# Projection and attention of an AdaLN block in one program block, with constant rows set four at a time

## What is computed

```
# B = 8 batches, C = 512 channels, T = 1024 tokens, H = 16 heads of 32
Q, K, V = proj(Wq), proj(Wk), proj(Wv)          # y = einsum('oc,bct->bto', W, x)
att = einsum('bhqd,bhkd->bhqk', Q, K) / sqrt(32) + b[0]
att = att * m + (1.0 - m) * -1e30               # m masks keys
y = softmax(att) @ V                            # (B, C, T) after transposes
q, in_scale = per_token_quant_int8(y)           # a "token" is a channel row of 1024
out = (q @ weight.T) * in_scale * w_scale + bias
x = x + out.astype(float16)
```

## Time and profile before

| | |
|---|---|
| median of 3 executions | 2441.13 us (2439.86 to 2441.28) |
| the profiled execution's own time | 2436.68 us |
| its span, first to last instruction | 2434.8 us |
| TensorE busy | 2381.2 us, 98% |
| GpSimd, VectorE, ScalarE busy | 1673.1, 1560.6, 1347.4 us |
| mean granted TensorE clock | 0.993 of 2.4 GHz |

### The profile page before, as it was taken

One profiled execution on the slowest core, in us unless ns is written; L12 is line 12 of the kernel. 1 busy time (PEld: TensorE's weight loads), 2 busy tenths in 40 slices (PEclk: granted clock), 3 DMA queues, 4 the chain that ended last, 5 costly groups with the idle time before them and its releaser, 6 DMA issues.

```text
span 2434.8 us, 37355 instructions
## 1 busy us (share of the span) xinstructions
PE 2381.2 (98%) x12344; PEld 1343.4 (55%) x12376; DVE 1560.6 (64%) x1683; ACT 1347.4 (55%) x2536; POOL 1673.1 (69%) x677
## 2 busy tenths in 40 slices
PE   8999999997999999999999999999999999999996
PEld 7888888884444444444444444444444444444442
DVE  3311111145777787777777777777777777777771
ACT  3322222214666666666666666666666666666664
POOL 3322223414788888888778888887888888888777
PEclk9999999998999999999999999999999999999999
DMA  6655555365677766776777776766776667766751
GB/s 242 255 193 205 211 195 196 149 211 131 149 160 159 159 148 153 161 158 154 156 158 160 156 161 152 159 148 154 158 161 156 153 151 160 159 155 152 157 111 46
DMA packets 143498, 396.55 MB, mean 163 GB/s; under 512 B 14584, under 2 KB 50424, under 8 KB 127296
## 3 DMA queue, kind: packets, MB, share of 16 engines
q0 software_dynamic: 18144, 132.13, 27.4%
q10 hardware_dynamic: 48864, 129.19, 22.0%
q1 hardware_dynamic: 76416, 134.34, 15.1%
HBM read 161.51 MB, written 100.93 MB: 108 GB/s over the span
## 4 chain that ended last, share of the span: by engine, by line
PE 64%; DMA 6%; issue 2%; DVE 2%; POOL 2%; SPq 0%; ACT 0%; ACTq 0%; POOLq 0%; DVEq 0%
PE score L724 21%; PE pv L751 18%; PE ring L128 17%; DMA q_stack<-max_lo 5%; PE ring L784 4%; PE ring L763 2%; PE ring L766 2%; DVE neg_max L137 1%; DMA k_stack<-bias_part 1%; PE ring L775 1%; POOL acc L1014 1%; DMA probs<-probs 0%; PE ring L144 0%; POOL acc L1026 0%; SPq L165 0%
## 5 line engine op out<-in xcount | busy, mean ns | idle before, releaser
L832 ACT ACTIVATE probs<-score 128x512 f32<-128x512 f32 x2048 | 1075.3, 604 | 583.2 <-PE score L724 570.3
L137 DVE TENSOR_REDUCE neg_max<-ring 128x1 f32<-128x1024 f32 x1024 | 1208.6, 1220 | 236.7 <-PE ring L128 225.1
L724 PE MATMUL score<-q_stack,k_stack 100*128 100x512 f32 x2048 | 875.4, 429 | 12.3 <-ACT probs L832 5.5
L1014 POOL TENSOR_TENSOR acc<-acc,probs 128x2048 f32<-128x2048 f32 x189 | 866.9, 4587 | 25.2 <-DMA probs<-probs 10.5
L128 PE MATMUL ring<-k_stack,q_stack 98*128 98x512 f32 x2048 | 810.6, 396 | 12.8 <-DMA k_stack<-bias_part 12.5
L724 PEld LDWEIGHTS score<-q_stack,k_stack 100*128 100x128 f32 x2048 | 387.4, 189 | 492.2 <-ACT probs L832 357.6
L751 PE MATMUL pv<-probs,v_in 128*32 128x512 f32 x4096 | 546.3, 605 | 0.0
L128 PEld LDWEIGHTS ring<-k_stack,q_stack 98*128 98x128 f32 x2048 | 390.7, 191 | 79.1 <-DMA k_stack<-bias_part 12.8
L1014 POOL TENSOR_TENSOR acc<-probs 128x2048 f32<-128x2048 f32 x63 | 289.0, 4588 | 105.0 <-DMA probs<-probs 105.0
L526 POOL TENSOR_TENSOR q_stack<-x_raw,k_stack 128x1024 fp32r<-128x1024 f32 x28 | 67.7, 2455 | 293.1 <-ACT k_stack L402 293.1
L998 POOL DMA_DIRECT2D probs<-probs x126 | 108.7, 863 | 170.2 <-PE pv L751 163.3
(11 more groups left out here) (101 smaller groups left out, 2028.9 us busy)
## 6 DMA issues: line engine op xcount, KB each, us to landing
probs<-probs POOLq DMA_DIRECT2D x126, 1024.0 KB, 8.0
q_stack<-qk_part ACTq DMA_DIRECT2D x183, 256.0 KB, 4.5
k_stack<-qk_part ACTq DMA_DIRECT2D x90, 512.0 KB
qk_part<-part_hi SPq DMA_DIRECT2D x64, 512.0 KB, 2.6
qk_part<-part_lo SPq DMA_DIRECT2D x64, 512.0 KB, 3.5
v_steps<-v_out SPq DMA_DIRECT2D x64, 256.0 KB, 2.2
v_out<-x ACTq DMA_DIRECT2D x32, 512.0 KB, 5.7
out<-v_out SPq DMA_DIRECT2D x64, 256.0 KB, 2.0
```

Source lines behind the costliest of these rows:

```text
L137: nc.vector.tensor_reduce(neg_max[:, pair // CHUNK, pair % CHUNK:pair % CHUNK + 1], ring[:, :], AX_X, ALU.max, negate=True).then_inc(neg_m ...
L724: pe.matmul(score[score_bank(t)][:, :], k_stack[par][0:ROWS, h, kt * P:(kt + 1) * P], q_stack[par][0:ROWS, half, h, :], start=True, stop=T ...
L832: nc.scalar.activation(probs[:, kt, h, :], score[score_bank(t)][:, :], ACT.Exp).then_inc(exp_done, 1)
L1014: nc.gpsimd.tensor_tensor(acc[:, half, :, :], first, probs[:, tile, :, :], ALU.add).then_inc(acc_done, 1)
```

## The change

Both parts are now written into one block, so the barrier between them is gone. What it ordered is ordered by semaphores: SyncE, VectorE and GpSimd begin attention with a wait for the last projection group (`proj_done`), ScalarE, VectorE and GpSimd with one for the last stores of `qk_part`; the first three score matmuls wait for `v_done`, and `V_BANKS` is turned so that bank 0 is the first to be free. `set_rows` writes rows 96 to 99 only, K's first, and the loads of rows 0 to 95 do not wait for it; the bias loads wait for K's rows. The load of V for step 0 is issued with the loads of step 0, before batch 7's stores; for this `v_in` exists throughout, and the projection's `w_raw` is a view of it.

```diff
@@ set_rows
-    nc.gpsimd.memset(q_stack[:, :, :, :].bitcast(F32), LIFT).then_inc(stack_set, 1)
-    nc.gpsimd.memset(k_stack[:, :, :].bitcast(F32), 1.0).then_inc(stack_set, 1)
+    nc.gpsimd.memset(k_stack[ROW_BIAS:ROWS, :, :].bitcast(F32), 1.0).then_inc(stack_set, 1)
+    nc.gpsimd.memset(q_stack[ROW_BIAS:ROWS, :, :, :].bitcast(F32), LIFT).then_inc(stack_set, 1)
@@ project
-        w_raw = sb("w_raw", [P, CT, C], F32)
+        w_raw = v_in[:, :, :, :].rearrange("p i a c -> p (i a c)").rearrange("p (a c) -> p a c", a=CT)
-        V_BANKS = (0, 1, 2)
+        V_BANKS = tuple((bank + SCORES - TT) % SCORES for bank in range(SCORES))
-        block = ctx.enter_context(nc.Block())
@@ project, SyncE, before batch 7
-            sp.wait_ge(stack_set, 2)
+            sp.wait_ge(proj_done, GROUPS * (B - 1))
             for k in range(3):
                 load_q(sp, qk_d, q_stack, 0, 0, 0, k, q1_loaded)
             for k in range(3):
                 load_k(sp, qk_d, k_stack, 0, 0, k, k_loaded)
+            sp.wait_ge(stack_set, 1)
             for part in range(2):
                 load_bias(sp, bias_d, k_stack, 0, 0, part, k_loaded)
             for k in range(3):
                 load_q(sp, qk_d, q_stack, 0, 0, 1, k, q2_loaded)
+            sp.wait_ge(fw_done, 1)
+            for i in range(2):
+                sp.wait_ge(v_stored[i], 16 * (B - 1) * TT // 2)
+            sp.dma_start(v_in[:, 0, :, :], v_d[0]).then_inc(v_loaded[0], 16)
             batch(B - 1, 1, last=True)
-            for i in range(2):
-                sp.wait_ge(part_stored[i], 32 * B * STAGES // 2)
@@ project, GpSimd, before batch 7
                     pool.wait_ge(proj_done, GROUPS * b)
+                    pool.wait_ge(k_lo_done, TT * b)
                     set_rows(nc, q_stack[0], k_stack[0], stack_set)
+                    pool.wait_ge(stack_set, 2)
@@ attend, SyncE
-            sp.dma_start(v_in[:, 0, :, :], v_d[0]).then_inc(v_loaded[0], 16)
-            sp.wait_ge(stack_set, 4)
+            sp.wait_ge(proj_done, PROJECTED)
             for k in range(3):
                 load_q(sp, qk_d, q_stack, 1, 1, 0, k, q1_loaded)
             for k in range(3):
                 load_k(sp, qk_d, k_stack, 1, 1, k, k_loaded)
+            sp.wait_ge(stack_set, 3)
@@ attend, TensorE
+                if isinstance(s, int) and s == 0 and t < SCORES:
+                    pe.wait_ge(v_done, B * TT - SCORES + 1 + t)
+                    if isinstance(own, int) and (own, pair) == (1, 0):
+                        pe.wait_ge(stack_set, 4)
@@ attend, ScalarE
-                if s == 0 and t == 24:
-                    act.wait_ge(stack_set, 4)
+            for i in range(2):
+                act.wait_ge(part_stored[i], 16 * B * STAGES)
@@ attend, GpSimd
+            pool.wait_ge(proj_done, PROJECTED)
+            for i in range(2):
+                pool.wait_ge(part_stored[i], 16 * B * STAGES)
             set_rows(nc, q_stack[1], k_stack[1], stack_set)
+            pool.wait_ge(stack_set, 4)
```

More of the change, by code:

```diff
@@ L68 @@
 MAX_ROWS = 16 * 2
+GROUPS = 3 * TT
+STAGES = 2 * CT
+PROJECTED = GROUPS * B
 def wait(eng, sem, value):
@@ L170, in project @@
             stack_set, k_loaded, q1_loaded, q2_loaded, rowmax_done, neg_max_done,
-            ident_set, maxT_done, max_hi_done, max_lo_done, max_rows):
+            ident_set, maxT_done, max_hi_done, max_lo_done, max_rows,
+            block, sems, v_in, v_loaded, proj_done, part_stored, v_done, fw_done):
     QHI, QLO, KHI, KLO = range(4)
@@ L209, in project @@
         k_lo_done = sem("k_lo_done")
-        v_done = sem("v_done")
-        part_stored = [sem(f"part_stored{i}") for i in range(2)]
         small_loaded = sem("small_loaded")
@@ L359, in batch @@
                 if last:
+                    pe.wait_ge(stack_set, 2)
                     pe.wait_ge(k_loaded[0], LOADS_K)
@@ L905, in _ @@
         def _(dve):
+            dve.wait_ge(proj_done, PROJECTED)
+            for i in range(2):
+                dve.wait_ge(part_stored[i], 16 * B * STAGES)
             nc.vector.memset(ones[:, :], 1.0).then_inc(const_set, 1)
@@ L1095, in program @@
         banks = score + [buf[:, half * N:(half + 1) * N] for buf in ring for half in range(2)] + [pv]
-        stack_set, rowmax_done, neg_max_done, ident_set, maxT_done, max_hi_done, max_lo_done = (
+        stack_set, rowmax_done, neg_max_done, ident_set, maxT_done, max_hi_done, max_lo_done, proj_done, v_done, fw_done = (
             ctx.enter_context(nc.semaphore(name)) for name in
-            ("stack_set", "rowmax_done", "neg_max_done", "ident_set", "maxT_done", "max_hi_done", "max_lo_done"))
-        k_loaded, q1_loaded, q2_loaded, max_rows, v_stored = (
+            ("stack_set", "rowmax_done", "neg_max_done", "ident_set", "maxT_done", "max_hi_done", "max_lo_done",
+             "proj_done", "v_done", "fw_done"))
+        k_loaded, q1_loaded, q2_loaded, max_rows, v_stored, v_loaded, part_stored = (
             [ctx.enter_context(nc.semaphore(f"{name}{i}")) for i in range(2)]
-            for name in ("k_loaded", "q1_loaded", "q2_loaded", "max_rows", "v_stored"))
+            for name in ("k_loaded", "q1_loaded", "q2_loaded", "max_rows", "v_stored", "v_loaded", "part_stored"))
+        sems = ctx.enter_context(ExitStack())
+        block = ctx.enter_context(nc.Block())
         shared = (banks, ring, q_stack, k_stack, neg_max, max_hi, max_lo, ident, v_out, v_stored,
                   stack_set, k_loaded, q1_loaded, q2_loaded, rowmax_done, neg_max_done,
-                  ident_set, maxT_done, max_hi_done, max_lo_done, max_rows)
+                  ident_set, maxT_done, max_hi_done, max_lo_done, max_rows,
+                  block, sems, v_in, v_loaded, proj_done, part_stored, v_done, fw_done)
         project(nc, x, mask, wqT, wkT, wvT, qk_d, v_d, bias_d, cond_b, fw, wT, ws_rep, fb_rep, w_scale, f_bias, *shared)
```

16 lines of the change are left out of this document (6 added, 10 removed).

## The result

The changed kernel takes 2426.36 us in the median (2425.51 to 2428.83, 5 executions) against 2439.86 us before (2438.3 to 2441.28, 5 executions): ratio 0.9947, 95% interval 0.9932 to 0.9961, 13.5 us less. The forecast was 2428.1 us, a gain of 13.0 us on the median of 2441.13 us known then.

A forecast was written before the change was run, and what follows sets the result against it. TensorE, busy 2381.2 of 2434.8 us, was taken as the bound; the border held 18.95 us, less a 3.6 us wait and 2.3 us dip gives 13.0 us gained, so 2428.1 us, own range 2425 to 2431, with A and B 2422 to 2434.7.

The forecast's parts named there:

- The border: Between projection and attention: idle time and half-clock stretches of TensorE hold 18.95 us, all this change can win.
- The barrier, 1.75 + 1.5 us: Between the two parts: removal gains 1.75 us of TensorE idling and 1.5 us of half clock behind it.
- Issue of the loads at 557.3: SyncE's first load of step 1 moves from 564.66 to about 557.3, right behind the last V store.
- The memset at its upper bound of 3.5 us: K's constant rows on GpSimd: begun at 556.2, taking at most 3.52 us, set at 559.7, costing nothing.
- Landing at 574.0, P + 18.3: Bias rows of step 1 land at 574.0, the loads keeping a 45% share beside GpSimd's transfers.
- Wait of 3.6 us and dip of 2.3: TensorE at t = 20 still waits 3.6 us for the bias rows, then loses 2.3 us at half clock.
- Sum 13.0 us: Whole kernel: 18.95 - 3.6 - 2.3 = 13.0 us gained, median 2428.1 us.
- Batch 7's stores: Projection's end: part stores go out earlier, ScalarE's 14.44 us wait ends 4.3 us sooner; hidden, no gain.
- 4 us of cover on the adds: GpSimd's first-half adds, read at t = 55, end by about 597 against a need at 601; nothing counted.
- A: Border: GpSimd's transfers hardly slow the loads, landing at 569.6, no wait left, all 18.95 us won, 2422.2; chance 0.12.
- B: Border: queues served packet by packet, bias rows land at 579.7, wait 9.3 us, gain 6.4 us, 2434.7; chance 0.18.
- D: Batch 7: step 0 loads and V delay part stores, TensorE stops at a K group, 2446 us or more; chance 0.04.

The follow-up runs named there:

- e4_pairs_held: The changed kernel with GpSimd's first pair of accumulating transfers of step 0 held until K of step 1 has landed; 2430.90 us, ratio 0.9961.
- e1_barrier_back: The changed kernel with the two blocks and the barrier between them put back; 2428.15 us, ratio 0.9954.
- e8_pairs_small: The changed kernel with the two accumulating transfers of step 0's first half cut to 16 of 512 columns per tile; 2422.29 us, ratio 0.9936.
- e9_v1_t34: The changed kernel with V for step 1 loaded at t = 34 of step 0 instead of t = 8; 2425.34 us, ratio 0.9946.
- e6_both: The changed kernel with GpSimd's first transfers held until K of step 1 lands and V for step 1 loaded at t = 22; 2427.93 us, ratio 0.9953.
- e5_v1_late: The changed kernel with V for step 1 loaded at t = 22 of step 0 instead of t = 8; 2426.35 us, ratio 0.9948.
- e11_barrier_and_held: The changed kernel with barrier back, V for step 1 at t = 34, GpSimd's second transfer held until step 0's row maxima land; 2430.61 us, ratio 0.9970.

## Why the prediction was right, step by step

The time came out right, and so did the path: the loads of step 1, issued earlier, shorten the wait at t = 20. How the loads share the DMA engines was wrong, and that the landing came within 1.4 us all the same was luck.

- **The border is all there is to win, and the 12.5 us wait is most of it**: right. Everything after the start of step 2 kept its length.
- **The barrier, 1.75 + 1.5 us**: the first right in the trace as a shift of TensorE's arrival, wrong as a gain. The sum let it vanish in the wait behind it, but did not say that it is worth nothing by itself, as the kernels with the barrier put back show at the border. The dip was read too large. In the change t = 0 to t = 8 takes 564.00 - 558.55 = 5.45 us at a granted clock of 1.00, not 4.95, partly because a row-max there waits for VectorE; so the dip before cost 6.47 - 5.45 = 1.0 us.
- **Issue of the loads at 557.3**: P + 1.6 was forecast and P + 1.5 measured. The memset at its upper bound of 3.5 us was right too.
- **Landing at 574.0, P + 18.3**: measured P + 19.5 to 19.7. The sum let the data of GpSimd's transfer flow 1.3 us after its issue, and took 45% as the share that the loads keep beside it. In the kernel before, GpSimd's transfer (q0) is issued at P + 12.3 and its first packet stands at P + 19.0. Until then the loads (q1) have the engines but for V; from then on they have little. The list of DMA queues of the kernel before, from 574.6 to 586.1 us:

```profile
q0 software_dynamic: 273, 2.10, 87.6%
q1 hardware_dynamic: 209, 0.69, 17.9%
```

So the 45% is the mean of two stretches of which neither has it. In the change q0's first packet stands at P + 15.0, 5.5 us after its issue, and by then the loads are nearly through. The same list of the changed kernel, first from 559.8 to 573.3 us, where q1 holds the loads and one V store, then from 573.3 to 577.7, up to P + 19.4:

```profile
q1 hardware_dynamic: 1394, 2.63, 81.5%
q10 hardware_dynamic: 101, 0.41, 11.7%
...
q0 software_dynamic: 110, 0.90, 98.4%
q10 hardware_dynamic: 43, 0.11, 9.7%
q1 hardware_dynamic: 14, 0.02, 1.8%
```

Three things make up the landing. The loads need almost 11 us of all engines, not 9.4, and alone they end at P + 14.5. V for step 1 (q10), beside them from P + 12.2, puts the last packet at P + 16.2 (e4_pairs_held). And beside GpSimd's transfer the last 14 packets of q1 drag on until P + 19.3; TensorE starts 0.4 us later. The experiments take these terms away one by one: 2.1 us of start for the transfers of GpSimd, 2.8 for V, 3.6 for both.

- **Wait of 3.6 us and dip of 2.3**: the wait was 4.4. The dip is less than the prediction's way of counting makes it: from the row-max after t = 20 to the score of t = 28 the kernels with the barrier back, where nothing waits and the clock is at 1.00, take 6.1 us, not 5.8, with a transposing matmul in between. So the dip was 8.6 - 6.1 = 2.5 us in the change, 1.7 in its second profile, and 2.8 instead of 3.2 before.
- **Sum 13.0 us**: 11.4 and 11.6 by the two profiles up to step 2, 13.5 and 13.6 by the medians. With the two dips as measured the border held 1.75 + 1.0 + 12.5 + 2.8 = 18.1 us, and less 4.4 and 2.5 the sum is 11.2. The forecast median came close by luck, through the 2 us that the border does not hold. The one profile of before has P = 555.7, near the low end of the 555.1 to 558.3 of the thirteen others, so a typical execution of before is likely slower than the one profiled; with a single profile of before this is not shown.
- **Batch 7's stores**: ScalarE's 14.44 us wait became 11.43 us and ended 3.1 us sooner from P; 4.3 was forecast. Hidden, as said.
- **4 us of cover on the adds**: the weak place was named, but not what it does. The adds are not waited for at t = 55; it seems that their lag delays the next transfers and through them the row maxima of step 1. With the adds ending up to 8.7 us after t = 36 step 1 kept its 57.2 us; from 9.5 us on it took 58.7 to 63.0. The change stands at 6.2 and 7.8.
- **Rivals**: A was out by the loads' own time and V. B's time was out, P + 24 was not reached, but its rate was right. The objection to it counted the first transfer's 144 packets, 6.6 us, from 569.3; from the first packet at 574.7 they end at 581.3, and GpSimd's add waited until 581.97. B failed because in the change the loads are nearly through before the two queues meet. While they do meet, 273 packets of q0 pass beside 209 of q1 in the kernel before, not far from one for one. To that extent the Trainium skill's rule ("DMA: Bandwidth & Descriptors", the paragraph on arbitration under queues, rings and completion order), which stood beside B, agrees with the trace, as far as the trace's packets are the ones it means. D did not occur.

## What to carry to other kernels

Before crediting the removal of a barrier or a wait, ask which arrival it lets you reach earlier and whether something else lands later than that: here the barrier's 3 us were free in both directions at the border, while 6 us in the issue of a load were worth 10. Don't read a queue's share over a long window as a rate: split the window where the other queue's first packet comes. Where transfers fill the DMA engines, the small late ones (here 8 KB of row maxima) are the next to be waited for, and making room for a large transfer by holding another only moves the queue: list what lands in the same 20 us, and who waits for each. To compare executions whose earlier parts vary, count from an event at the border, not from the start.

## What the runs showed of the hardware

- A GpSimd memset of 4 x 4096 took 3.51 us, one of 128 x 4096 took 3.52 us.
- The two stores of 8 KB after t = 23 of step 0 took from 3.0 to 7.9 us to land after issue; the DMA share from issue to landing was 0.87 or more where they took over 5.4 us, and 0.65 to 0.90 where they took less.
- The length of a wait did not tell whether the clock falls. Of the sixteen waits of TensorE of 1.2 to 2.6 us between P and the end of t = 32 of step 0, twelve had the granted clock at 0.50 behind them. Four had it at 1.00 throughout: 1.7 us at the barrier (e1_barrier_back), 2.4 us at t = 20 (e8_pairs_small), 2.6 us and 1.7 us at t = 32 (e4_pairs_held, e9_v1_t34). The 0.6 us at t = 20 of e6_both left it at 1.00 too. A dip behind 2.2 us cost 2.5 us up to t = 36 in e6_both and 1.1 in e5_v1_late.
- With nothing beside them but a V store, the last packet of the loads ended 1.4 us before the matmul that waits for the bias rows.
- The first packet of GpSimd's accumulating transfer came 1.6 us after its issue when the DMA engines were idle (e4_pairs_held, e6_both) and 3.7 to 6.7 us after it in the ten kernels that issue it well inside the loads; in e11_barrier_and_held, where it is issued at P + 12.3 and the loads end at 15.6, it came after 1.6 us as well.
